# A conditional four-layer MLP chain on one Trainium2 core: order of the last blocks, of the last layer's matmul and of the output transfers

## The reference, cut to what matters

```python
x = x + _L0_cond_ref(...)   # linear layer with a mixture of LoRA terms
x = x + _L1_cond_ref(...)   # sum_e w_e * (gelu(x Wg_e) * (x Wu_e)) Wd_e, the 2 best experts, + a shared one; inner width 512
x = x + _L2_cond_ref(...)   # one expert: (silu(x Wu + bu) * (x Wg + bg)) Wd + bd; inner width 256
x = x + _L3_cond_ref(...)   # x @ sum_g y[b,g] * (weight[g] * mask) + bias
```

## Time and profile before

| | |
|---|---|
| time, median of 3 runs | 73.73 us |
| lowest and highest | 73.14 and 74.64 us |
| profiled execution, its own time | 73.86 us |
| its span, first to last instruction | 72.1 us |
| granted TensorE clock, mean | 0.993 |
| PE busy | 68.0 us (94%) |
| ACT busy | 48.7 us (68%) |
| DVE busy | 45.6 us (63%) |
| POOL busy | 36.3 us (50%) |

### The profile page before, as it was taken

One profiled execution on the slowest core, in us unless ns is written; L12 is line 12 of the kernel. 1 busy time (PEld: TensorE's weight loads), 2 busy tenths in 40 slices (PEclk: granted clock), 3 DMA queues, 4 the chain that ended last, 5 costly groups with the idle time before them and its releaser, 6 DMA issues.

```text
span 72.1 us, 1068 instructions
## 1 busy us (share of the span) xinstructions
PE 68.0 (94%) x316; PEld 55.0 (76%) x316; DVE 45.6 (63%) x83; ACT 48.7 (68%) x96; POOL 36.3 (50%) x50
## 2 busy tenths in 40 slices
PE   4998999999999999999999999999999999999930
PEld 4995867887787788778777877887788778788720
DVE  0255778577655567765555776555977576958940
ACT  0836879466787666678766667879677995576640
POOL 3020484044999999866999986655540600000000
PEclk9999999999999999999999999999999999999997
DMA  0896999999400000000000000000000000000025
GB/s 2 220 364 257 324 379 368 413 423 409 197 0 9 0 0 0 0 0 0 5 5 0 0 0 0 0 9 0 0 0 0 0 0 0 0 0 0 0 111 180
DMA packets 2884, 6.62 MB, mean 92 GB/s; under 512 B 448, under 2 KB 1728, under 8 KB 2880
## 3 DMA queue, kind: packets, MB, share of 16 engines
q1 hardware_dynamic: 2304, 6.05, 22.5%
q10 hardware_dynamic: 576, 0.52, 2.2%
HBM read 6.04 MB, written 0.52 MB: 91 GB/s over the span
## 4 chain that ended last, share of the span: by engine, by line
PE 94%; DVE 1%; ACT 1%; issue 1%; DVEq 0%
PE gp L433 9%; PE gp L429 9%; PE gp L430 9%; PE acc L433 9%; PE acc L430 9%; PE acc L429 9%; PE up L433 9%; PE up L429 9%; PE up L430 9%; PE up L410 4%; PE acc L425 1%; PE up L578 1%; PE acc L458 1%; PE gp L539 1%; PE gp L416 1%; DVE res L684 1%
## 5 line engine op out<-in xcount | busy, mean ns | idle before, releaser
L356 ACT ACTIVATE act<-gp 128x512 f32<-128x512 f32 x24 | 14.4, 598 | 11.8 <-PE gp L433 11.5
L265 POOL TENSOR_TENSOR wlo<-raw_skill,whi 128x384 fp32r<-128x384 f32 x16 | 16.3, 1017 | 7.9 <-ACT whi L329 7.7
L642 DVE TENSOR_TENSOR hlo<-up,hhi 128x512 fp32r<-128x512 f32 x27 | 18.4, 682 | 1.9 <-ACT hhi L344 1.9
L635 DVE SCALAR_TENSOR_TENSOR up<-up,gate_w,act 128x512 f32<-128x512 f32 x16 | 12.1, 759 | 11.1 <-ACT act L356 11.0
L344 ACT ACTIVATE hhi<-up 128x512 fp32r<-128x512 f32 x27 | 16.0, 593 | 2.8 <-DVE up L628 2.6
L429 PE MATMUL acc<-hhi,whi 128*128 128x512 f32 (+1 forms) x28 | 11.2, 400 | 0.0
L429 PE MATMUL gp<-xhi,whi 128*128 128x512 f32 x27 | 11.2, 414 | 0.0
L433 PE MATMUL acc<-hlo,whi 128*128 128x512 f32 (+1 forms) x28 | 10.8, 387 | 0.0
L430 PE MATMUL acc<-hhi,wlo 128*128 128x512 f32 (+1 forms) x28 | 10.8, 386 | 0.0
L429 PE MATMUL up<-xhi,whi 128*128 128x512 f32 x27 | 10.7, 395 | 0.0
L433 PE MATMUL up<-xlo,whi 128*128 128x512 f32 x27 | 10.7, 394 | 0.0
(11 more groups left out here) (109 smaller groups left out, 93.6 us busy)
## 6 DMA issues: line engine op xcount, KB each, us to landing
raw_skill<-skill SPq DMA_DIRECT2D x4, 768.0 KB, 6.7
raw_shared<-shared SPq DMA_DIRECT2D x4, 192.0 KB, 3.6
w3in<-l SPq DMA_DIRECT2D x1, 576.0 KB, 5.5
raw_l<-l SPq DMA_DIRECT2D x1, 386.5 KB, 7.7
raw_l<-l_folded SPq DMA_DIRECT2D x1, 386.5 KB, 7.5
x<-x_t ACTq DMA_DIRECT2D x2, 128.0 KB, 3.1
x<-x_t SPq DMA_DIRECT2D x1, 256.0 KB, 3.7
out_t<-res SPq DMA_DIRECT2D x1, 256.0 KB, 2.1
```

The source lines that it names most:

```text
L265: pool.tensor_tensor(wlo[:, p, c], raw_piece(p)[:, c], whi[:, p, c], ALU.subtract).then_inc(s_wlo, 1)
L356: sc.activation(act[:, k % 2, :], gp[k % PAIRS][:, :], ACT.Gelu_apprx_tanh).then_inc(s_act, 1)
L635: ve.scalar_tensor_tensor(out=out, in0=u, scalar=gate_w[:, b, r:r + 1], in1=a, op0=ALU.mult, op1=ALU.mult).then_inc(s_h, 1)
L642: ve.tensor_tensor(hlo[:, i, t], hidden_of(k, t), hhi[:, i, t], ALU.subtract).then_inc(s_hlo, 1)
```

## The change

- PE: gate and up of 27 stand directly behind those of 26, then down 25, then `l3_of_x2`. `down_by_halves(k)` becomes `down_half(k, n)`. Batch 0's last matmul (line 578) moves from in front of down 26 to between the two halves of down 27.
- ACT: silu 27 goes in front of the high part of 26. `x3` is made here, between the two halves of the high part of 27. The first half of batch 1's result goes in front of batch 0's. ACT issues the transfer of the second half of batch 1.
- DVE: `x3` is gone. The first half of hidden 27 goes in front of the low part of 26.
- SP: first the transfer of the first half of batch 1, then that of batch 0.

```diff
         @block.sync
+            sp.wait_ge(s_res1[0], 1)
+            sp.dma_start(out_t[:, T:T + HALF], res[:, 1, :HALF]).then_inc(s_out, 16)
             sp.wait_ge(s_res0, 1)
             sp.dma_start(out_t[:, 0:T], res[:, 0, :]).then_inc(s_out, 16)
-            sp.wait_ge(s_res1[1], 1)
-            sp.dma_start(out_t[:, T + HALF:], res[:, 1, HALF:]).then_inc(s_out, 16)
             sp.wait_ge(s_out, 16 * 3)
         @block.scalar
             silu(N1 + 2)
+            silu(N1 + 3)
             h_hi(N1 + 2)
-            silu(N1 + 3)
-            for i in range(2):
-                h_hi(N1 + 3, slice(i * HALF, (i + 1) * HALF))
-            sc.wait_ge(s_l3o, 1)
-            sc.activation(res[:, 0, :], l3out0, ACT.Identity, bias=bias3).then_inc(s_res0, 1)
+            h_hi(N1 + 3, slice(0, HALF))
+            sc.wait_ge(s_bias02, 1)
+            sc.wait_ge(s_d, N1 + 2)
+            sc.activation(x3[:, 0, :], acc[0][:, :], ACT.Identity, bias=bias02[:, :]).then_inc(s_x3, 1)
+            h_hi(N1 + 3, slice(HALF, T))
             sc.wait_ge(s_bias31, 1)
             sc.wait_ge(s_d, N)
             sc.activation(res[:, 1, :HALF], y1[0], ACT.Identity, bias=bias31[:, :]).then_inc(s_res1[0], 1)
-            sc.wait_ge(s_res1[0], 1)
-            sc.dma_start(out_t[:, T:T + HALF], res[:, 1, :HALF]).then_inc(s_out, 16)
+            sc.wait_ge(s_l3o, 1)
+            sc.activation(res[:, 0, :], l3out0, ACT.Identity, bias=bias3).then_inc(s_res0, 1)
+            sc.wait_ge(s_res1[1], 1)
+            sc.dma_start(out_t[:, T + HALF:], res[:, 1, HALF:]).then_inc(s_out, 16)
         @block.tensor
-            def down_by_halves(k):
+            def down_half(k, n):
 
                 p, i = piece_of(k), k % HBUFS
                 wait_down(k)
-                for n in range(2):
-                    t = slice(n * HALF, (n + 1) * HALF)
-                    ...
+                t = slice(n * HALF, (n + 1) * HALF)
+                ...
             gate_up(N1 + 2, fresh_input=True)
+            gate_up(N1 + 3)
+            down(N1 + 1)
             l3_of_x2()
-            down(N1 + 1)
-            gate_up(N1 + 3)
-
+            down_half(N1 + 2, 0)
+            down_half(N1 + 2, 1)
+            down_half(N1 + 3, 0)
             pe.wait_ge(s_f3, N_F3)
             pe.wait_ge(s_x3, 1)
             pe.wait_ge(s_hlo, N1 + 2)
             pe.matmul(l3out0, w3[:, 0, :], x3[:, 0, :], start=True, stop=True).then_inc(s_l3o, 1)
-            down_by_halves(N1 + 2)
-            down_by_halves(N1 + 3)
+            down_half(N1 + 3, 1)
         @block.vector
-            def x3_sum():
-                ve.wait_ge(s_bias02, 1)
-                ve.wait_ge(s_d, N1 + 2)
-                ve.tensor_scalar(x3[:, 0, :], acc[0][:, :], bias02[:, :], None, ALU.add).then_inc(s_x3, 1)
             hidden(N1 + 2)
-            x3_sum()
+            hidden(N1 + 3, slice(0, HALF))
             h_lo(N1 + 2)
-            halves = [slice(i * HALF, (i + 1) * HALF) for i in range(2)]
-            for t in halves:
-                hidden(N1 + 3, t)
-            for t in halves:
-                h_lo(N1 + 3, t)
+            hidden(N1 + 3, slice(HALF, T))
+            h_lo(N1 + 3, slice(0, HALF))
+            h_lo(N1 + 3, slice(HALF, T))
```

More of the change, by code:

```diff
@@ L514, in down @@
                 lo_pass(out, whi[:, p, 2 * P:], hlo[:, i, :], is_last(k), residual=True).then_inc(s_d, 1)
-            def down_by_halves(k):
+            def down_half(k, n):
                 p, i = piece_of(k), k % HBUFS
                 wait_down(k)
-                for n in range(2):
-                    t = slice(n * HALF, (n + 1) * HALF)
[L522 to L528, removed]
+                t = slice(n * HALF, (n + 1) * HALF)
+                if k == N - 1:
+                    pe.wait_ge(s_hhi, k + 1 + n)
+                hi_passes(y1[n], whi[:, p, 2 * P:], wlo[:, p, 2 * P:], hhi[:, i, t], False)
+                pe.wait_ge(s_hlo, k + 1 + (n if k == N - 1 else 0))
+                mm = lo_pass(y1[n], whi[:, p, 2 * P:], hlo[:, i, t], is_last(k))
+                if n or k == N - 1:
+                    mm.then_inc(s_d, 1)
             def fold_down3():
```

## The result

| | before | changed |
|---|---|---|
| time, median of 6 executions each | 73.55 us | 75.31 us |
| lowest and highest | 73.14 and 74.64 | 74.37 and 75.71 |
| ratio to before, 95% interval | | 1.0163 [1.0104, 1.0222] |
| the profiled execution's own time | 73.86 | 74.75 |
| its span, first to last instruction | 72.1 | 71.9 |

The ratio is taken over the fast executions alone and the median over all six, which is why 75.31 / 73.55 is more than the ratio; the ratio is 1.2 us.

A forecast was written before the change was run, and what follows sets the result against it. PE, busy 68.0 of 72.1 us, and the results' way to memory were taken as the bound. PE and results -0.07 plus transfers +0.36 gave +0.29 us: 74.15 on the profiled 73.86, 74.0 for the median, range 73.2 to 74.8.

The forecast's parts named there:

- PE's list: PE's reordered tail: without stall its last matmul ends at 69.08 instead of 69.17, 0.09 us earlier.
- The hand-overs: ACT and DVE passing results of blocks 26 and 27: first low half of 27 has no margin, stall 0.02 us.
- The third rival: Block 27's low part comes late and PE stops for it, up to 0.4 us: 74.2 to 74.4; chance 0.12.
- The outputs: Result transfers at the end: the 256 KB issued 0.67 us later, sharing one stream with the last 128 KB, +0.36 us.
- 2.2 or more: Sign that the forecast is right: landing time in us of the last 128 KB transfer, issued by ACT.
- The sum for the tail: PE and results -0.07 us, output transfers +0.36 us, together +0.29 us.
- my 69.10: Forecast end of PE's last matmul: 69.08 plus 0.02 us of stall, 0.07 earlier than before.
- the fourth rival: A stop of PE in the tail lowers its clock, doubling the 1.21 us from 67.87 on: 75.2 us; chance 0.02.
- The sum: Whole kernel: +0.29 us on the profiled 73.86 gives 74.15; for the median 74.0, 0.4% slower.
- my cases: The forecast of two last transfers in one full stream, chance 0.58, and its rivals; they lie between 73.7 and 74.6 us.
- a slower stream: Last output bytes moving at 307 GB/s, the lower bound, 1.28 us instead of 1.11: +0.17 us.
- the scatter of the runs: Single executions of the kernel before spread from 73.14 to 74.64 us; half of this was allowed a median.

The follow-up runs named there:

- e3: The changed kernel with `x3` computed on DVE again, behind the low part of 26; ratio to before 1.0328.
- e13: The changed kernel without the repeated waits of `down_half` and without batch 0's 256 KB output transfer; ratio to before 0.9934.
- e6: The changed kernel without the two redundant waits that `down_half` repeats, order of all matmuls unchanged; ratio to before 1.0068.
- e5: The kernel before with one redundant wait on PE behind the warm-up matmuls; ratio to before 1.0015.
- e12: The kernel before with one redundant wait on PE at gate and up of block 12; ratio to before 0.9968.
- e10: The kernel before with one redundant wait on PE in front of its last three matmuls; ratio to before 1.0010.
- e1: The kernel before with the issuers of the two 128 KB output transfers exchanged, ACT issuing the last; ratio to before 1.0009.
- e14: The kernel before with one redundant wait on PE in gate and up of each of blocks 1 to 23; ratio to before 1.0094.

## Why the prediction was right or wrong

- **PE's list:** 5.08 us from the start of the tail was forecast and 5.03 measured. A 256-column matmul added 0.113 on average in fifteen places (65.76 to 67.46), where I had 0.117. Nothing was late.
- **The hand-overs:** right to a few hundredths, with 0.36 taken off for the earlier start. Silu 27: forecast 64.40, measured 64.40. High part of 26: 64.98 and 64.98, so its place behind silu 27 costs nothing. `x3`: 66.02 and 66.01, and 0.67 long where I took 0.68. Low part of 27, first half: its end 67.06 and 67.02. The third rival, a late chain of block 27, did not happen; e3 shows that its mechanism is real, 0.66 us with `x3` on DVE.
- **The outputs:** batch 0's transfer was issued at 69.07 (forecast 69.18), ACT's at 69.30 (69.35), with a landing time of 2.2 ("2.2 or more"). The mechanism is right and e13 confirms it. The sum for the tail was +0.29, measured +0.16. The difference arises in front of batch 0's issue, which comes 0.11 earlier behind the start of the tail than forecast: line 581 ends 0.07 earlier (0.05 from the faster matmuls, and my 69.10 had 0.02 of stall), and ACT took up the float32 result 0.04 behind its end in the chain (68.32 to 68.36), where I had put 0.09. The rest is rounding.
- **The clock:** no sign of the fourth rival; it was granted in full up to the span's end.
- **The step that failed** is in "The sum": "On the profiled execution's 73.86 that is 74.15". It carries the 1.76 us outside the span over unchanged. They became 2.85. The profiled pair adds up with it: +1.09 outside, -0.36 for the earlier start of the tail, +0.16 in the tail, +0.89 in all (73.86 to 74.75). None of my cases had a mechanism outside the span. The median of all executions, 75.31, lies outside the range of 73.2 to 74.8. By the ratio the changed kernel is at 74.75 (73.55 x 1.0163), just inside its upper end, and that is luck: the upper end was made of a slower stream, a late chain and the scatter of the runs, and none of them made the loss. Without the two waits (e6) the ratio is 1.0068 [1.0024, 1.0113], where my 74.0 was 1.004 of the 73.73.
- The two waits stood in the diff for everyone to see: `down_half` calls `wait_down` for each half, where `down_by_halves` called it once. I costed waits by who waits for what and not by the place that they take in a program. The block loads at 23 and 48 us, 25 apart, could be read from the trace of before. They would have been a warning that a next one may fall at 73 to 74, right at the end; they could not have said that it comes, since e5 and e12 have 710 instructions and no third load.
- **The direction:** the forecast was the same within 2% and 0.4% slower. 1.6% slower is four times as much, and with 2.2% as the interval's upper end it is not settled that it is within 2%.

What stays open is which property of PE's program brings the load, and whether the 0.9 us are the load's or have a cause in common with it. In the kernels here one instruction more brings a late load when it stands in the last 30 of the list (in e10 only that of 8 KB) and none when it stands further ahead; with 23 more, ahead, the load comes earlier and only 0.13 us go with it.

## What to carry to other kernels

Compare the time less the span between two profiles before explaining anything from the spans: here three quarters of the loss was in that difference, and no view of the engines shows it. Look for the instruction loads in the DMA view, behind the span's end too: if one stands there that the kernel before does not have, try without redundant waits on the engine with the longest program. The spacing of the loads tells only where one may come. And a transfer that is moved later shares its bytes with those that end the kernel: two that are last together end when the stream of both is through.

## What the runs showed of the hardware that I had not expected

- A code load of 16 KB 1.7 us behind the last profiled instruction goes with 0.9 us more (2.71 against 1.81 outside); 1.0 us behind it, with 0.13 (1.92 against 1.79).
- One redundant wait behind the warm-up matmuls moved PE's block loads from 23 and 48 us to 19 and 43 to 44 us; one in the middle of the list moved none.
- The outside of one kernel is nearly constant when there is no load (1.74 to 1.84 over 29 executions) and scatters with one (2.35 to 2.98 over the four kernels that have the 16 KB load late).
- Who issues a transfer of 128 KB, SP or ACT, makes no difference that can be measured here: in e1 the last one, issued by ACT, lands in 1.9 us as SP's did before, and the ratio is 1.0009.
- 23 more waits in the list of PE, which is busy 94% of the span, went with 0.5 us more of span (72.1 against 71.6, e14).
